# Cross-attention after an adapter layer: row copies as a stage of their own, key turns one per query block, group exits and first key weights in halves, block clearing held until the last h

## What is computed

```python
# layer 0: adapter with a router over 8 experts
w = softmax(x @ router_W.T + router_b)            # (b, s, 8)
a_sum = einsum('bsh,arh->bsr', ctx_as_lora_A, ...)  # rank 64, summed over 4
y = einsum('bsr,nhr->bsnh', a_sum, lora_B)
h = nan_to_num(x + 0.5 * einsum('bsn,bsnh->bsh', w, y), nan=0, posinf=1e4, neginf=-1e4)
# layer 1: masked cross-attention to the same context, residual, layer norm
Q, K, V = h @ Wq.T + bq, ctx @ Wk.T + bk, ctx @ Wv.T + bv
attn = softmax(where(mask, Q K^T / sqrt(32), -inf))
z = h + (attn V) @ Wo.T + bo
out = (z - mean) / sqrt(var + 1e-5) * ln_g + ln_b
```

## Time and profile before

| | us |
|---|---|
| median of 3 runs | 701.13 |
| lowest, highest | 699.31, 701.17 |
| profiled execution, device time | 699.19 |
| its span, first to last instruction | 697.4 |
| TensorE busy in it | 669.2 |
| VectorE busy in it | 498.4 |
| ScalarE, GpSimd busy in it | 295.4, 208.9 |
| mean granted TensorE clock | 0.988 |

### The profile page before, as it was taken

How to read it: one execution, slowest core, us unless ns; L and a number is a source line. 1 busy time by engine, 2 the same in 40 slices (tenths; PEclk the granted TensorE clock), 3 DMA queues, 4 the chain that set the end, 5 groups by cost and what they waited for, 6 DMA issues and landing times.

```text
span 697.4 us, 10734 instructions
## 1 busy us (share of the span) xinstructions
PE 669.2 (96%) x3615; PEld 573.4 (82%) x3615; DVE 498.4 (71%) x948; ACT 295.4 (42%) x891; POOL 208.9 (30%) x215
## 2 busy tenths in 40 slices
PE   8999889999999999999798999999999999999995
PEld 6878667788788888888677898888888888888884
DVE  5779882567835785577835777888888888888734
ACT  4622321302122122310215675766666666666511
POOL 0300000200020000200403333456665566656652
PEclk9999989999999999999999999999999999999999
DMA  9965675313776347651346797353545244523211
GB/s 310 316 228 166 194 229 137 150 48 90 241 246 237 92 146 247 213 180 46 150 126 180 251 414 246 77 173 93 162 111 163 76 144 119 167 87 110 105 69 69
DMA packets 101062, 115.18 MB, mean 165 GB/s; under 512 B 41360, under 2 KB 75280, under 8 KB 101008
## 3 DMA queue, kind: packets, MB, share of 16 engines
q1 hardware_dynamic: 101008, 114.50, 50.4%
HBM read 68.33 MB, written 46.14 MB: 164 GB/s over the span
## 4 chain that ended last, share of the span: by engine, by line
PE 83%; DVE 10%; issue 2%; ACT 2%; SPq 2%; DMA 1%; POOL 0%; DVEq 0%; ACTq 0%
PE ps L539 24%; PE ps L541 24%; PE ps L540 24%; PE ps L681 4%; PE ps L590 3%; PE ps L622 2%; DVE w_lo L745 1%; DVE q_sb L852 1%; DMA stage<-WkT 1%; DVE h_t L839 1%; DVE x_sb L826 1%; PE ps L602 1%; DVE pos L831 1%; DVE h_t L842 1%; SPq L346 1%
## 5 line engine op out<-in xcount | busy, mean ns | idle before, releaser
L539 PE MATMUL ps<-act_hi,w_hi 128*128 128x512 f32 x256 | 103.9, 406 | 3.6 <-DVE q_sb L852 2.2
L539 PE MATMUL ps<-wo_hi,cx_hi 128*128 128x512 f32 x256 | 104.5, 408 | 0.0
L1053 ACT ACTIVATE s_sb<-s_sb,s_min 128x64 f32<-128x64 f32 x256 | 86.3, 338 | 42.3 <-DVE s_min L878 42.3
L540 PE MATMUL ps<-act_lo,w_hi 128*128 128x512 f32 x256 | 101.6, 397 | 0.0
L541 PE MATMUL ps<-act_hi,w_lo 128*128 128x512 f32 x256 | 101.5, 396 | 0.0
L541 PE MATMUL ps<-wo_hi,cx_lo 128*128 128x512 f32 x256 | 100.2, 392 | 0.0
L1116 POOL TENSOR_TENSOR u_sb<-a_sb,w_sb 128x512 f32<-128x512 f32 x16 | 21.9, 1392 | 261.5 <-DVE w_sb L796 256.2
L540 PE MATMUL ps<-wo_lo,cx_hi 128*128 128x512 f32 x256 | 100.2, 391 | 0.0
L1025 ACT ACTIVATE act_hi<-h_t 128x512 fp32r<-128x512 f32 x32 | 20.2, 633 | 164.9 <-DVE h_t L842 164.9
L1134 POOL TENSOR_TENSOR s_sb<-s_sb,s_min 128x256 f32<-128x256 f32 x64 | 39.3, 614 | 147.3 <-DVE s_min L878 147.3
L873 DVE SCALAR_TENSOR_TENSOR s_sb<-ps,mask_f 128x512 f32<-128x512 f32 x64 | 44.2, 691 | 51.8 <-PE ps L541 50.0
(11 more groups left out here) (110 smaller groups left out, 1521.1 us busy)
## 6 DMA issues: line engine op xcount, KB each, us to landing
q_cols<-q_sb SPq DMA_DIRECT2D x32, 512.0 KB, 4.5
qb<-q_cols SPq DMA_DIRECT2D x64, 256.0 KB, 3.5
x_sb<-xT SPq DMA_DIRECT2D x32, 256.0 KB, 3.0
h_rows<-hn_sb SPq DMA_DIRECT2D x32, 256.0 KB, 3.0
output_weights<-wo_sb SPq DMA_DIRECT2D x32, 256.0 KB, 2.8
z_sb<-h_rows SPq DMA_DIRECT2D x16, 512.0 KB, 4.1
out<-z_sb SPq DMA_DIRECT2D x15, 512.0 KB, 2.9
stage<-WkT SPq DMA_DIRECT2D x8, 512.0 KB, 6.3
```

Source lines behind the costliest of these rows:

```text
L539: pe.matmul(dst, lh, rh, start=(first and j == 0), stop=False)
L540: pe.matmul(dst, lh, rl, start=False, stop=False)
L1053: act.activation(s_sb[c % 4][:, h, :], s_sb[c % 4][:, h, :], ACT.Exp, bias=s_min[c % 2][:, h:h + 1], scale=-1.0, accum_out=s_sum[c % 2][:, ...
```

## The change

Seven edits. The row copy leaves `update` and becomes the stage `copy`, on VectorE alone, directly behind `rows`; at chunk 6 of batch 0 it now stands ahead of `values_out`, which stands ahead of `update`. The four key turns stand one behind each of four query steps, where they stood in pairs, and the order of the first query group is 0, 1, 5, 4, 6, 7, 2, 3, so that Q2 and Q3 are split last. A group's exit is split into two halves of two banks, each in a high and a low stage; behind the second group of a batch a `select` stands between the halves. The weights K0, K1 and K2 are loaded and split in two halves, and TensorE does banks 0 and 2 first. `expand(0, 0)` stands one key step later, and V1 is split ahead of `keys_out`. `WARM` is 11. GpSimd's clearing waits for the last h and no longer for the last update product.

```diff
-WARM = 15
+WARM = 11
-Q_FIRST = (0, 1, 5, 6, 7, 4, 3, 2)
+Q_FIRST = (0, 1, 5, 4, 6, 7, 2, 3)
+HALVED = 3
+def leave(i, g, part):
+    return [("exit_high", i, g, part), ("exit_low", i, g, part)]
-    def up(i, c, *between):
-        return ([("rows", i, c - 2)] if c >= 2 else []) + [("update", i, c)] + list(between) + [("select", i, c)]
+    def up(i, c, between=(), ahead=()):
+        return ([("rows", i, c - 2), ("copy", i, c - 2)] if c >= 2 else []) + [*ahead, ("update", i, c), *between, ("select", i, c)]
+    for n in range(HALVED):
+        out += [("half", n, 0), ("context_in", n), ("half", n, 1), ("keys", n)]
-    out += [("keys", 4)] + split("K", 7) + [("keys", 5), ("expand", 0, 0)] + split("V", 0) + [("keys", 6), ("keys", 7), ("keys_out",)]
-    out += [("expand", 0, 1)] + split("V", 1, 2) + [("values", 0)] + split("V", 3)
+    out += [("keys", 4)] + split("K", 7) + [("keys", 5)] + split("V", 0) + [("keys", 6), ("expand", 0, 0), ("keys", 7)] + split("V", 1)
+    out += [("keys_out",), ("expand", 0, 1)] + split("V", 2) + [("values", 0)] + split("V", 3)
-    out += [("values", KC - 1), ("values_out",)] + up(0, 6, *split("Q", 5)) + up(0, 7, *split("Q", 6))
+    out += [("values", KC - 1)] + up(0, 6, split("Q", 5), [("values_out",)]) + up(0, 7, split("Q", 4))
-    beside = {0: {0: split("Q", 7), 1: rows(0, 6) + split("Q", 4), 2: [("turn", 0), ("turn", 1)], 3: rows(0, 7) + [("turn", 2), ("turn", 3)],
-                  4: split("Q", 3), 5: [("mask",), ("route", 1)] + split("Q", 2)}}
+    beside = {0: {0: split("Q", 6), 1: rows(0, 6) + split("Q", 7) + [("turn", 0)], 2: [("turn", 1)], 3: rows(0, 7) + [("turn", 2)],
+                  4: [("turn", 3)] + split("Q", 2), 5: [("mask",)] + split("Q", 3) + [("route", 1)]}}
...
         held = out.pop()
-        out += [("query", i, 1, KC - 1), ("query_out", i, 1), held]
-        for c in range(KC - 1 - late, KC):
-            out += up(i + 1, c)
+        out += [("query", i, 1, KC - 1)] + leave(i, 1, 0) + [held]
+        if late:
+            out += up(i + 1, KC - 2, leave(i, 1, 1))
+        else:
+            out += leave(i, 1, 1)
+        out += up(i + 1, KC - 1)
...
-    left[5] += [("query_out", NB - 1, 0)]
+    left[4] += [("exit_high", last, 0, 0)]
+    left[5] += [("exit_low", last, 0, 0)] + leave(last, 0, 1)
...
+            def load_half(n, half):
+                cols = slice(half * HALF, (half + 1) * HALF)
+                sp.dma_start(stage[n][:, cols], w_v["K"][n][:, cols]).then_inc(half_in[n][half], 16)
...
-                for g in range(4):
+                for g in (0, 2, 1, 3) if halved else range(4):
+                    if halved and g == 1:
+                        pe.wait_ge(stage_lo, k + 1)
...
+            def copy(i, c):
+                copy_h_rows(KC * i + c)
...
             def zero():
-                pool.wait_ge(up_mm, ALL)
+                pool.wait_ge(h_ready, ALL)
```

More of the change, by code:

```diff
@@ L144, in run, with exits @@
             stages[what](*index)
-def exits(i, g):
-    return (2, 3, 0, 1) if (i, g) == (NB - 1, 0) else (0, 1, 2, 3)
+def exits(i, g, part):
+    order = (2, 3, 0, 1) if (i, g) == (NB - 1, 0) else (0, 1, 2, 3)
+    return [(place, order[place]) for place in (2 * part, 2 * part + 1)]
 def live(n, total):
@@ L288, in xattn_kernel @@
         stage_in = [sem(f"stage_in{k}") for k in range(4)]
+        half_in = [[sem(f"half_in{n}{half}") for half in range(2)] for n in range(HALVED)]
+        half_hi, half_lo = sem("half_hi"), sem("half_lo")
         stage_hi, stage_lo = sem("stage_hi"), sem("stage_lo")
@@ L404, in store_q, with exit_low @@
                              q_sb[n % 4][:].bitcast(F32).rearrange("p l t -> p (l t)")).then_inc(q_stored[n % 4], 16)
-            def query_out(i, g):
-                for place, j in enumerate(exits(i, g)):
+            def exit_low(i, g, part):
+                for place, j in exits(i, g, part):
                     store_q(KC * i + 4 * g + j, KC * i + 4 * g + place)
@@ L627, in query @@
                     pe.wait_ge(stage_lo, PLACE["Q", k] + 1)
-                    first, last = k == 0, k == 2
+                    first, last = k == Q_FIRST[0], k == Q_FIRST[-1]
                 else:
@@ L632, in query @@
                     pe.wait_ge(hlo_done, KC * i + k + 1)
-                for j in range(4):
+                for _, j in exits(i, g, 0) + exits(i, g, 1) if last else enumerate(range(4)):
                     if first:
@@ L947, in step @@
                         stage_(n)
-            run({"context_in": context_in, "adapter": adapter, "split": split, "keys_out": keys_out, "turn": turn,
-                 "values_out": values_out, "mask": mask_addend, "route": router, "expand": expand, "update": update,
-                 "select": select, "flush": flush, "query_out": query_out, "pair_out": pair_out, "output_weight": output_weight,
+            run({"context_in": context_in, "adapter": adapter, "half": half, "split": split, "keys_out": keys_out, "turn": turn,
+                 "values_out": values_out, "mask": mask_addend, "route": router, "expand": expand, "copy": copy, "update": update,
+                 "select": select, "flush": flush, "exit_low": exit_low, "pair_out": pair_out, "output_weight": output_weight,
                  "step": step})
@@ L1098, in step @@
                         stage_(n)
-            run({"context_in": context_in, "split": split, "turn": turn, "values_out": values_out, "route": router_exp,
-                 "expand": expand, "select": select, "query_out": query_out, "pair_out": pair_out,
+            run({"context_in": context_in, "half": half, "split": split, "turn": turn, "values_out": values_out, "route": router_exp,
+                 "expand": expand, "select": select, "exit_high": exit_high, "pair_out": pair_out,
                  "output_weight": output_weight, "step": step})
```

70 lines of the change are left out of this document (45 added, 25 removed).

## The result

The changed kernel takes **697.29 us** (median of 6 runs, 695.56 to 698.89), the kernel before beside it 700.6 (6 runs): a ratio of 0.9958, 95% interval 0.994 to 0.9976, or some 2.9 us less. A second set, run later beside the combinations, gave 697.07 (12 runs) and a ratio of 0.9957 (0.9936 to 0.9978). The forecast was 698.4 with a sum of -2.7, so total and sign were right.

The account below looks back on a forecast made before the run. TensorE, busy 669.2 of 697.4 us, bounds the kernel, so only its pauses can be won. The terms 0+1.9-0.6-3.0+1.2-2.2 sum to -2.7 us; against the median of 701.13 that gives 698.4, range 694.8 to 701.3.

Parts of the forecast that it names:

- Start: First weights in halves, fewer warm-up products: the first product may start earlier, but route(0) waits for x; 0 us.
- V1's split: V1 split ahead of the key copies: first value step later (+0.65), clock falls behind a 2.7 us pause (+1.2); +1.9 us.
- Row copy: Copy ahead of the values' exit fills VectorE's idle hole; the first pause merges into one ahead of turn(1); -0.6 us.
- Turns: One key turn per query step, Q2 and Q3 split last: pauses of 1.6 and 1.4 us go; -3.0 us.
- Exits in halves: Behind batch 1 VectorE idles 1.3 us between exit halves, so TensorE pauses 1.2 for the row copy; +1.2 us.
- the pause of 2.0: In batch 3: halved exits remove it by letting two banks go a query step earlier.
- Clearing: GpSimd's clearing held until the last h: masks regain 4.6 us, scores(4) comes 3.4 earlier, a clock fall costs 1.2; -2.2 us.
- scores(4), pause of 3.3: TensorE stops some 3.3 us at scores(4) for a query load in SyncE's launch row, and the clock falls: +1.2.
- (A): Rival: the clock doesn't fall at the two new pauses, 2 x 1.2 less, 696.0 us; 12%.
- (B): Rival: SyncE's queue sets x's landing; x, K4 and V1 come 3.0 us later and the clock falls, 702.6 us; 8%.
- (C): Rival: the halves delay x by 1.3 us and the clock falls wholly or partly ahead of route(0), 700.5 us; 25%.
- (D): Rival: VectorE finds room ahead of turn(1) and V1's copies cost nothing, -8.8 us, 692.3 us; 10%.

Follow-up runs that it names:

- the combinations: The changed kernel with V1's split later, group exits whole, first turn earlier and scores(4)'s query load earlier: 684.54 us; the same without the query load edit: 685.73 us.

## Why the prediction was right

The mechanisms hold point by point; the sizes don't, and the total came out closer than its terms deserve.

- **Start, 0.** Right in kind: `route(0)` at 18.56 and 18.67 with a first product 1.4 apart. By the times -1.2, within the error.
- **V1's split, +1.9.** The place was right, the size wrong. The step that failed is "TensorE has no work [...] 2.7 us [...] so +1.2": the pause was 3.5, since V1 landed 0.5 later than before, and the low clock lasted 6.8 and not 3.4. (In the second profile of the changed kernel it lasted 3.4, so part of the miss is chance.) Update (0, 0) starts at 50.41 where it started at 46.63, +3.8. Undone, the edit gives 4.3.
- **Row copy, -0.6.** "One pause of some 7 us stands where two of 3 stood": right. By the run without it the edit is worth -0.2 with an error of 2; nothing is shown to be won.
- **Turns, -3.0.** Both pauses are gone. Pairing the turns again gives back the first one and 1.5. That Q2 and Q3 come last was not tried alone; its pause of 1.5 ahead of the last query step is absent from every one of these traces.
- **Exits in halves, +1.2.** The hold is 1.28 and the pause 1.0, near the forecast. The run without the halves puts their cost at 3.0, both batches together. The forecast for that is 2.5: 1.2 here and, in the clearing's sum, the 1.3 by which the hold moves SyncE's row. Two pauses were in no sum, the 1.3 at 188.1 in place of 1.0, and one of 0.6 at 294.2, 0.3 in the kernel before. That one is there with whole exits too and is 0.3 again with the start as before; its cause isn't found. The halves in batch 3, to which the prediction gave the end of the pause of 2.0, were undone in no run; the pause is gone.
- **Clearing, -2.2.** Right in kind. With the hold of 1.3 taken out it stands for -3.5, and -2.5 is measured: beside the clearing the pause grew by 3.6 and not 4.6, and part of that came back at scores(0) and scores(4).
- **scores(4), pause of 3.3.** 2.9, and shown to be SyncE's row by moving one load. The wait of 1.5 at scores(0) for the first key loads, in the same row, was missed.

The terms, each measured by undoing it, are -1.2 + 4.3 - 0.2 - 1.5 + 3.0 - 2.5 = +1.9, and with -1.5 for the Q order +0.4. The change as a whole measures -2.9. They needn't agree: each figure carries 2 us, and all six share the error of the changed kernel's own ratio. Exits and clearing and SyncE's row act on one wait, and a pause shortened in one place changes whether the clock falls in another. What part each of these has in the difference of 3.3 stays open. That the forecast total met the measured one is thus partly luck: V1's term was too small by 2.4 by the times, and no term is shown that makes up for it.

Of the rivals, (A) was out in the profiled execution of the changed kernel, where the clock fell at both new pauses, and in the second one; elsewhere it was a matter of luck (pauses of 2.1 to 2.8 at scores(4) without a fall in four of the experiments' traces, one of 2.8 at the first value step in another). (B) and (C) were out by 18.56. (D) was dismissed for a wrong reason, "VectorE's 2.93 of 3.00": the room was there, in the order of its queue and in the 1.65 of idleness just ahead of the window, and its two parts, the second turn and V1's copies, gave 4.7 and 4.3 once the order was changed, where its sum had 4.2 and 1.9 for them.

## What to carry to other kernels

A busy engine in the other's pause doesn't mean that it has no room: look at what it is busy with, and whether the one result that is waited for could stand ahead in its queue. An in-order queue makes each early item a delay for all behind it; moving one exit, one split, one launch gave 2 to 5 us each here, in sum more than the whole change. Price a new pause of 3 us or more with the clock's fall behind it, as 1 to 3 us more on TensorE, one of 2 to 3 with the same as a matter of chance, and read the mean granted clock of all runs beside each time: part of the difference between two single traces is only that.

## What the runs showed of the hardware

- A pause of TensorE and the clock behind it, over the 13 profiled executions (pauses by the distance between starts, less one product): all 21 of 3.0 us or more had the clock at its low level in them or from at most 0.5 behind them on; of 16 between 2.0 and 3.0 it was 10, up to 1.3 behind them; of those below 2.0, down to 1.0, none. Pauses of 2.9 and 2.8 passed without a fall, and two of 2.1 to 2.2 didn't. The prediction had taken a fall behind 2.0 as certain from one case. The Trainium skill, "TensorE: Matmul & The Clock Gate", Part 1, says that the moment of a change isn't tied to the kernel. These runs agree: the same pause of 2.9 at the second turn had a fall behind it in two executions and none in a third.
- The low stretches were 3.4, 6.8 and once 10.2 us long (105.2 to 115.4 in the run with the query load first). Behind the same pause of 6.9, those of 6.8 cost different amounts, depending on how much of them lay in the pause itself: 10 products in 99.97 to 106.80, 15 in 105.87 to 112.69.
- A mask on VectorE took 3.99 us, through two MEMSETs of GpSimd, where its own time is 0.43.
- One and the same load, V1's, launched by the same code behind the same loads, landed between 38.9 and 41.6 us in eight executions.
